# Third layer's attention: TensorE turns the weights of one batch and the context of the batch two ahead in turn

## The reference, cut to what matters

```python
nx = layer_norm(x, ln_gamma, ln_beta)
q = nx @ Wq
k = prototype_bank @ Wk            # prototype_bank: the context, 32 x 1444 x 128
v = prototype_bank @ Wv
scores = einsum('bth,bph->btp', q, k) * H ** (-0.5)
weights = softmax(scores, axis=-1)
evidence = einsum('btp,bph->bth', weights, v)
```

## Time and profile before

| | us |
|---|---|
| median of 3 runs | 6407.64 (6407.46 to 6416.72) |
| the profiled execution | 6396.8 |
| its span, first to last instruction | 6395.0 |
| TensorE busy in the span | 5146.5 (80%) |
| VectorE busy | 4097.1 (64%) |
| ScalarE busy | 2978.6 (47%) |
| GpSimd busy | 1581.0 (25%) |
| mean granted TensorE clock | 0.866 |

### The profile page before, as it was taken

How to read it: one execution, slowest core, us unless ns; L and a number is a source line. 1 busy time by engine, 2 the same in 40 slices (tenths; PEclk the granted TensorE clock), 3 DMA queues, 4 the chain that set the end, 5 groups by cost and what they waited for, 6 DMA issues and landing times. The chain is left out here.

```text
span 6395.0 us, 151199 instructions
## 1 busy us (share of the span) xinstructions
PE 5146.5 (80%) x63886; PEld 3314.4 (52%) x63886; DVE 4097.1 (64%) x7828; ACT 2978.6 (47%) x4342; POOL 1581.0 (25%) x869
## 2 busy tenths in 40 slices
PE   3837999999964839999999757779575699999996
PEld 2614555555542615666666435555352366666663
DVE  5546888888855527777777642324455477777784
ACT  1323666666642315666666522212222366666663
POOL 2024444444312032233222110000301322322221
PEclk7657999999986659999999877769765799999998
DMA  3425555555403434555555111110151555555540
GB/s 72 69 45 161 161 162 162 162 162 162 148 7 63 70 106 156 169 163 162 168 170 171 51 27 51 47 38 1 37 83 28 151 178 168 163 163 172 171 130 15
DMA packets 559421, 726.21 MB, mean 114 GB/s; under 512 B 195354, under 2 KB 471994, under 8 KB 546362
## 3 DMA queue, kind: packets, MB, share of 16 engines
q1 hardware_dynamic: 547226, 701.17, 37.8%
q10 hardware_dynamic: 11520, 15.37, 1.0%
HBM read 450.42 MB, written 264.09 MB: 112 GB/s over the span
## 5 line engine op out<-in xcount | busy, mean ns | idle before, releaser
L1227 DVE TENSOR_REDUCE maxima<-ps 100x1 f32<-100x482 f32 (+1 forms) x4608 | 2719.1, 649 | 889.9 <-PE ps L1072 880.3
L1182 ACT ACTIVATE probs<-ps 128x800 f32<-128x800 f32 (+1 forms) x2304 | 1800.9, 835 | 654.2 <-PE ps L1093 652.5
L1072 PE MATMUL ps<-kst,qst 48*100 48x482 bf16 (+1 forms) x4608 | 1114.3, 410 | 107.9 <-DMA qst<-cross_q_parts 51.5
L1279 POOL TENSOR_TENSOR kparts<-kf,zero 128x1444 bf16<-128x1444 f32 x192 | 498.3, 2595 | 2273.9 <-ACT kf L1154 2243.9
L1110 PE MATMUL ps<-probs,vals 128*9 128x100 f32 x36864 | 1012.5, 250 | 7.9 <-ACT probs L1182 0.8
L1093 PE MATMUL ps<-qst,kst 128*128 128x200 bf16 (+1 forms) x9216 | 999.6, 250 | 10.6 <-DMA qst<-nparts 4.3
L1093 PEld LDWEIGHTS ps<-qst,kst 128*128 128x128 bf16 (+1 forms) x9216 | 759.0, 98 | 250.3 <-issue 124.9
L1110 PEld LDWEIGHTS ps<-probs,vals 128*9 128x9 f32 x36864 | 734.3, 90 | 259.7 <-issue 219.3
L1072 PEld LDWEIGHTS ps<-kst,qst 48*100 48x100 bf16 x4608 | 341.1, 119 | 627.5 <-DVE maxima L1227 328.4
L1160 ACT ACTIVATE vals<-ps 128x512 f32<-128x512 f32 (+1 forms) x288 | 162.1, 563 | 465.8 <-PE ps L1055 465.8
L1044 PE MATMUL ps<-ident,ctok 128*128 128x128 f32 (+1 forms) x1152 | 194.6, 290 | 213.8 <-DMA ctok<-in_ctx_dram 110.1
(11 more groups left out here) (251 smaller groups left out, 5193.9 us busy)
## 6 DMA issues: line engine op xcount, KB each, us to landing
kst<-ctx_k_stack SPq DMA_DIRECT2D x96, 2888.0 KB
ctx_k_stack<-kparts SPq DMA_DIRECT2D x192, 541.5 KB
ctx_k_stack<-kparts SPq DMA_DIRECT2D x192, 361.0 KB
ctok<-in_ctx_dram SPq DMA_DIRECT2D x96, 704.0 KB
ctx_k_stack<-kparts SPq DMA_DIRECT2D x192, 180.5 KB
c<-in_ctx_dram SPq DMA_DIRECT2D x32, 704.0 KB
o_sums<-osb SPq DMA_DIRECT2D x96, 200.0 KB
qst<-cross_q_parts SPq DMA_DIRECT2D x1152, 12.5 KB
```

Source lines behind the costliest of these rows:

```text
L1072: nc.tensor.matmul(ps[0:N, at:at + w], g.qst[s][row0:row0 + CROWS, j, N * e:N * e + N], g.kst[s][row0:row0 + CROWS, j, a:a + w], start=Tru ...
L1182: nc.scalar.activation(probs[kt % 2][hf][0:kts[kt], :].rearrange("p (k n) -> p k n", k=2), src, ACT.Exp).then_inc(exp_done, 1)
L1227: nc.vector.reduce_max(maxima[:, col:col + 1], ps[0:N, at:at + widths[c]], AX.X).then_inc(m_read, 1)
L1279: return nc.gpsimd.tensor_tensor(out, src, g.zero[0:src.shape[0], 0:1].to_broadcast(list(src.shape)), ALU.add)
```

## The change

Only TensorE's order in this phase is changed. The turns are taken out of pe_scores and pe_evidence into two functions of one group each, and the order of a round becomes: weights of b, groups 1 and 2; context of b + 2, groups 1 and 2; weights of b, group 3; context of b + 2, group 3; evidence of b; scores of b + 2. Every group keeps the waits that it had. Batches 0 and 1 still turn their context right in front of their scores, and the rounds of batches 30 and 31 have no context to turn.

```diff
--- before.py
+++ after.py
@@ -1557,16 +1557,19 @@
             sp.dma_start(ctok[s][:, 0:full, :], g.ctx[bass.ds(b, 1), 0:128 * full, :].rearrange("a (k p) c -> p (a k) c", p=P)).then_inc(ctx_loaded[s], 16)
             sp.dma_start(ctok[s][0:kts[-1], full, :], g.ctx[bass.ds(b, 1), 128 * full:S, :].rearrange("a p c -> p (a c)")).then_inc(ctx_loaded[s], 16)
 
+        def pe_turn_context(pe, k, t):
+            b, s, r = k.b, k.s, k.r
+            if t == 0:
+                wait(pe, ctx_loaded[s], 32 * (r + 1))
+            wait(pe, t_read, 3 * b + max(t - 1, 0))
+            for i, kt in enumerate(range(4 * t, 4 * t + 4)):
+                o = T_BANK + BANK * (t % 2) + 128 * i
+                n = kts[kt]
+                ins = nc.tensor.transpose(ps[:, o:o + n], ctok[s][0:n, kt, :], g.ident[0:n, 0:n])
+            ins.then_inc(t_full, 1)
+
         def pe_scores(pe, k):
             b, s, r = k.b, k.s, k.r
-            wait(pe, ctx_loaded[s], 32 * (r + 1))
-            for t in range(3):
-                wait(pe, t_read, 3 * b + max(t - 1, 0))
-                for i, kt in enumerate(range(4 * t, 4 * t + 4)):
-                    o = T_BANK + BANK * (t % 2) + 128 * i
-                    n = kts[kt]
-                    ins = nc.tensor.transpose(ps[:, o:o + n], ctok[s][0:n, kt, :], g.ident[0:n, 0:n])
-                ins.then_inc(t_full, 1)
             wait(pe, u_ready, b + 1)
             wait(pe, t_read, 3 * (b + 1))
             wait(pe, exp_done, b)
@@ -1576,16 +1579,19 @@
                 ins = nc.tensor.matmul(ps[0:N, a:a + w], ub[s][:, :], ctxT[s][:, a:a + w], start=True, stop=True)
             ins.then_inc(s_full, 1)
 
+        def pe_turn_weights(pe, k, t):
+            b, s, r = k.b, k.s, k.r
+            if t == 0:
+                wait(pe, p_norm, b + 1)
+            wait(pe, p_read, 3 * b + max(t - 1, 0))
+            for i, kt in enumerate(range(4 * t, 4 * t + 4)):
+                o = P_BANK + BANK * (t % 2) + N * i
+                n = kts[kt]
+                ins = nc.tensor.transpose(ps[0:n, o:o + N], pq[s][:, 128 * kt:128 * kt + n], g.ident[0:N, 0:N])
+            ins.then_inc(p_full, 1)
+
         def pe_evidence(pe, k):
             b, s, r = k.b, k.s, k.r
-            wait(pe, p_norm, b + 1)
-            for t in range(3):
-                wait(pe, p_read, 3 * b + max(t - 1, 0))
-                for i, kt in enumerate(range(4 * t, 4 * t + 4)):
-                    o = P_BANK + BANK * (t % 2) + N * i
-                    n = kts[kt]
-                    ins = nc.tensor.transpose(ps[0:n, o:o + N], pq[s][:, 128 * kt:128 * kt + n], g.ident[0:N, 0:N])
-                ins.then_inc(p_full, 1)
             wait(pe, p_read, 3 * (b + 1))
             wait(pe, e_read, b)
             for kt, n in enumerate(kts):
@@ -1672,18 +1678,23 @@
 
             @block.tensor
             def _(pe):
-                pe_scores(pe, known(0))
-                pe_scores(pe, known(1))
-                pe_evidence(pe, known(0))
-                pe_scores(pe, known(2))
-                for i in range(loops):
-                    for u in range(1, LAG + 1):
-                        pe_evidence(pe, at(i, u))
-                        pe_scores(pe, at(i, u + 2))
-                for b in range(LAG * loops + 1, B):
-                    pe_evidence(pe, known(b))
-                    if b + 2 < B:
-                        pe_scores(pe, known(b + 2))
+                for b in range(2):
+                    for t in range(3):
+                        pe_turn_context(pe, known(b), t)
+                    pe_scores(pe, known(b))
+                for b in range(B):
+                    k, k2 = known(b), known(b + 2) if b + 2 < B else None
+                    for t in range(2):
+                        pe_turn_weights(pe, k, t)
+                    if k2 is not None:
+                        for t in range(2):
+                            pe_turn_context(pe, k2, t)
+                    pe_turn_weights(pe, k, 2)
+                    if k2 is not None:
+                        pe_turn_context(pe, k2, 2)
+                    pe_evidence(pe, k)
+                    if k2 is not None:
+                        pe_scores(pe, k2)
 
             @block.scalar
             def _(act):
```

## The result

The changed kernel takes 6256.48 us (median of 4 runs, 6249.39 to 6269.7), the kernel before beside it 6408.63 (6407.46 to 6416.72): a ratio of 0.9762, 95% interval 0.9744 to 0.9781, some 152 us less. The profiled execution took 6258.94 us, its span is 6257.1.

What follows compares the result with a forecast made beforehand. TensorE was taken as the bound, losing 97.5 us idle and much work at its low clock. Thirty rounds going from 15.49 to 10.89 us save 138 us from 6407.6, giving 6270 us, range 6245 to 6350.

Steps and rivals of the forecast that it cites:

- The wait on ScalarE: Third context group waits for ScalarE's first copy, behind the exponentials: starts no earlier than 4.23 us, evidence at 4.65.
- The load: TensorE waits for context b+2 at its first turn: load taken as 4.7 us, turns begin 2.33 us into the round.
- the sum: Full-clock round: 4.75 us up to evidence, 3.02 of evidence, 2.47 of scores, together 10.24 instead of 12.11.
- rival 4: The context load sets the round, binding from 5.6 us of loading up; below 6245 us or the load: 0.04.
- The round at full clock: A round of the 30-round loop at clock 1.00 was to take 10.24 us instead of 12.11.
- The clock: TensorE's clock falls in one round of four at 2.61 us, adding 0.65 us for a 10.89 us round.
- a fall should be over before or early in the scores: Gapless evidence and score matmuls restore the clock, so a fall costs only evidence at low clock, 2.61 us.
- The argument from density: The new 4.75 us stretch of turns is 68% busy, near the two-thirds-busy context stretch that never loses the clock.
- Rival 1: Clock falls every round and returns only within the scores: some 14.0 us a round, 6363 us; chance 0.24.
- rival 2: Idle time returns whole at the new waits: 15.4 to 15.7 us a round, 6405 to 6414 us; chance 0.05.
- rival 3: Clock stays low for the whole loop: 15.87 to 16.2 us a round, 6429 us, slower; chance 0.05.
- The rule by which the clock doesn't engage for transposes: Skill rule that turns don't count as busy: the 4.75 us would be idle, clock falling every round, 6329 us or rival 1.

Runs made afterwards that it cites:

- experiment 1: The changed kernel with a fourth context buffer, so each load is issued one round earlier: 6301.5 us, ratio 0.9838.
- experiment 6: Changed kernel, ScalarE's first two context copies before the exponentials, TensorE turning weights 3 after context 1 to 3: 6224.8 us with four context buffers, 6289.2 with three.
- experiment 5: The changed kernel with every context loaded first into an unread spare buffer, so the needed load lands later: 6349.4 us in one execution.
- experiment 2: The kernel of experiment 1 plus 8 identity turns a round behind the first two groups of context: 6247.9 us, ratio 0.9752.
- experiment 3: The kernel before, order unchanged, plus 8 identity turns a round behind the second group of weights: 6339.3 us, ratio 0.9899.
- experiment 4: The changed kernel without interleaving: three groups of weights, three of context, evidence, scores: 6290.8 us, ratio 0.9819.
- experiment 7: Four-buffer kernel of experiment 6, all ScalarE context copies before exponentials, VectorE's weight copies before the next maximum, TensorE in the changed kernel's order: 6192.0 us, ratio 0.9669.

## Why the prediction was right

The forecast was 6270 us, with 6245 to 6350 around it; 6256.5 was measured. By its steps:

**The wait on ScalarE**, priced from the one place at the start of the stage where the order already was as it would become: third group of context at 4.23 us, measured 4.18. That it sets the round at full clock, and the load does not, is shown by experiments 1 and 6.

**The load:** first turn at 2.33 us, measured 2.23. The prediction has two paths from there to evidence that do not agree: 2.41 us through TensorE's queue and VectorE's copies in the sum ("together 4.75"), 1.63 us through ScalarE's copy in rival 4. Measured is 2.16, through the queue (experiment 5). So "it binds from 5.6 us up" was too generous: the slack was 0.45 us and not 0.9. And the 4.75 us of the sum were the load's path, which in the changed kernel would end at 2.23 + 2.16 = 4.39, while ScalarE's, put at 4.65, ends last at 4.84: that the sum came within 0.1 us is in part luck.

**The round at full clock:** 10.24 predicted, 10.36 measured. The term that was mis-sized on the path that decides is the issue of the third group: 0.42 us predicted to the start of evidence, 0.66 measured (3877.89 to 3878.55). The scores took 2.50 instead of 2.47, evidence 3.02 as said.

**The clock:** one fall in four rounds at 2.61 us each was the term I had the least for, and both its factors were wrong in opposite directions. There were 3 falls in 30, and two of them cost 4.79 us, the third 1.25: 0.36 us a round instead of 0.65, so the total owes something to luck here too. The failed step is "a fall should be over before or early in the scores". Evidence and scores of a fallen round:

```profile
4054.97:4060.59 5.62, 5.62 (x25) 5.26 (x24) 0.27 (x1) 0.52 (x1) 0.00 (x0) 0.50 0.00 0
4060.59:4065.04 4.45, 4.45 (x7) 1.71 (x7) 0.26 (x1) 0.00 (x0) 0.00 (x0) 0.56 0.58 166
```

TensorE is busy without a gap for 10 us, and the clock stays at 0.50 through all of evidence and nearly all of the scores. Gapless was not enough.

**The argument from density** pointed the right way. Experiments 2 and 3 support it: turns that compute nothing, put into the gaps, leave far fewer rounds without the clock. But the busy share of the stretch of turns is too coarse a measure, as I used it. It is the same in two kernels, 2.75 us of 4.64 in the changed one and in experiment 1:

```profile
3873.91:3878.55 4.64, 2.75 (x25) 2.11 (x23) 3.89 (x8) 2.53 (x4) 0.35 (x1) 1.00 0.31 94
```
```profile
3898.36:3903.00 4.64, 2.75 (x24) 2.07 (x23) 4.39 (x8) 2.53 (x4) 0.35 (x1) 1.00 0.33 99
```

and yet the first lost the clock in 3 rounds of 30, the second in 17 (the row is of a round that lost it right after). What differs is where the gaps lie: one of 1.38 us early and one of 0.51 in the changed kernel, 0.89 and 1.01 later in experiment 1. That points to their place, but no run isolates it: experiment 1 moved the transfer too, and experiment 2, which keeps the moved transfer and the clock, fills a gap and does not move it. By which rule the clock falls is open.

**Where the gain is.** Per round: 12.11 to 10.36 us at full clock, 1.75 us or 52 us in all, from taking the turns out from between evidence and scores; and the loss to the clock from 3.38 (15.49 - 12.11) to 0.36 us, 91 us. The second, which I had put at 2.73 us a round, is the larger part, and experiment 3 shows that it can be had for two thirds (60 us) without any change of order. Whether the last third comes from the gap between evidence and scores, which is still there in experiment 3, was not tested by itself.

**The rivals.** Rival 1 (the clock falls in every round) is out by the 27 rounds at 1.00; rival 2 by the mean round of 10.72 us, rival 3 by the mean clock of 0.96; rival 4 by experiment 1. The rule by which the clock doesn't engage for transposes (the Trainium skill, TensorE: Matmul & The Clock Gate, Part 4: PE-mode transpose) is contradicted here for f32 turns: the only added instructions in experiments 2 and 3 were turns, and the mean clock rose from 0.84 to 0.99 and from 0.73 to 0.89.

## What to carry to other kernels

When TensorE's clock in a stage lies between its two levels, split the stage into rounds and compare the round at full clock with the mean: the one is the schedule, the other the clock, and a reordering can be worth more through the second. To price a wait that a new order makes, look for a prologue or an epilogue where the order is already so. And before removing a wait that is hidden, look at which gaps its removal leaves: an earlier load with no cost on any path cost 45 us here, and eight turns a round that compute nothing gave them back; better still is to remove the waits behind it too, engine by engine, until TensorE is the only bound.

## What was not expected of the hardware

In one fallen round of the changed kernel, 24 evidence and 6 score instructions without a gap, 10 us, did not bring the high clock back until their end (0.50, then 0.56), while kernels with f32 turns in their gaps kept it more often. And the falls come in patterns that repeat: the kernel before goes through its six rounds of 92.19 us again and again, once with a round left out; experiment 1 repeats 10.36, 13.6, 13.6 with one exception, and experiment 4 ends with six times 15.3, 11.6 and, but for the last time, two rounds of 10.5. A small change in a round can therefore move the total by far more than itself: 0.11 us a round at full clock, but 34 us in all, in experiment 4. Why the four runs of the changed kernel spread over 20 us is not shown; those of experiment 7, which never loses the clock, spread over 3.5, but those of experiment 4, which loses it in 14 rounds of 30, over 5.
